# Attention scores and exponents as float32r limbs in 32-row tiles, with three exponent banks and one accumulator

## The chip, the cores and the metric

One core of one Trainium2 chip. The time is device microseconds of one launch; the figure of a kernel is the median of its runs. The kernel before took 2334.4 us (three runs, 2331.25 to 2337.49).

## What is computed

Four sequences of 1024 tokens with 128 features, all float32, go through four layers, each with a layer norm before it and a residual sum after it: attention a, a mixture of experts, attention b, and the same experts again.

```python
# attention a: 16 heads of 8
Q, K, V = (content @ W).reshape(b, n, 16, 8)          # for Wq, Wk, Wv
alpha = softmax(einsum('bqhd,bkhd->bhqk', Q, K) / sqrt(8))
alpha = where(causal, alpha, 0)                       # masked after the softmax
Y = einsum('bhqk,bkhd->bqhd', alpha, V)
# attention b: q and k turned by rotary tables, softmax over all keys, no mask,
# then an output projection with a bias
# experts: 8 routed SwiGLU experts, the best 2 per token by softmax + bias, and a shared one
```

In attention a the denominator of the softmax runs over all keys, also the masked ones.

## The kernel before, in words

`build` runs the stages one after another, each in a block of its own: `setup`, `project` and `attend` for a, `route` and `experts`, `project` and `attend` for b, `project_out`, `route` and `experts`. Engines are held together by semaphores alone.

**Groups.** A sequence's 16 heads are four groups (`g`) of four heads (`hh`); with four sequences a layer has 16 groups (`n`). `project` makes q and k in 8 chunks of 512 tokens, splits each into three bfloat16 parts (ScalarE copies, L464 and L468; VectorE's subtraction, L445; POOL's, L413), and SP stores the parts and v in DRAM (`store`, L366 to L378). `load_group` (L269) brings a group back: the parts of q and k stacked so that one matmul over 96 rows gives the sum of all products of parts. The 32 scores of group 0 are already made at the end of `project` (L503 to L509, and L448).

**Maxima.** `score` (L298): for a head and a tile of 128 queries two matmuls of 512 keys each into one of the two slots of `ps_two`, which VectorE reduces to the negated maximum over 1024 keys (`take_max`, L308). The 32 columns of maxima of a group are transposed (`turn_max`, L808), copied (L747), split into three bfloat16 parts by POOL (`split_max`, L658) and put by DMA as rows 96 to 98 beside q (L641); the matching rows of k hold ones. That way the second matmul (`exponents`, L863), keys on the output's partitions and 512 queries on its columns, gives score minus maximum.

**Exponentials and weighting.** ScalarE exponentiates each 128x512 result (L731) from two banks of `ps_one` into one of four buffers of `probs`. `weigh` (L841) multiplies v (8 columns, and a ninth of ones for the denominator) with it in float32, the four heads in the four 32-column strips of the array, 256 queries at a time, summed over all 8 key tiles in the two banks of `ps_sum`. In layer a the part below the diagonal needs the ones column alone (`w01`), POOL multiplies the diagonal tile with the causal mask (L687), and pairs of probability tiles are added by POOL (L677), so that one matmul does for both where only the denominator is wanted. ScalarE copies the sums (L718), TensorE transposes them (L815), VectorE divides (L753, L755) and adds or stores (L763, L765).

**Order.** TensorE's order is written out by hand in `body` (L849): per step one exponent matmul, then what stands in `uses` for the step (a unit of scores for a later group, 40 steps ahead; the sums; the maxima), the second exponent matmul, and a quarter of `weigh` of the key tile before. A group has 32 steps (`STEPS`). VectorE follows the same list. An exponent matmul waits for the exponential two before it (L862), a score for the reduction two before it (L803). SP loads the group three ahead once the group before has been weighed (L648, L649). The groups of one sequence are written out; over the sequences runs a loop (`over_groups`, L626), as over the chunks (`over_chunks`).

## Time and profile before

| | |
|---|---|
| median of three runs | 2334.4 us (2331.25 to 2337.49) |
| span of the profiled execution | 2335.9 us; no other time of this execution is given |
| instructions | 45054 |
| TensorE busy, matmuls | 2088.4 us, 89% |
| TensorE weight loads, beside them | 905.2 us, 39% |
| VectorE busy | 1747.2 us, 75% |
| ScalarE busy | 1402.6 us, 60% |
| POOL busy | 557.9 us, 24% |
| DMA | 69.96 MB, mean 30 GB/s |

How to read it: busy shares are means over stages with different limits. Matmuls are pipelined and their ends are modelled, so the distance between two starts tells more than a duration. L12 is line 12 of the kernel; PEld is TensorE's weight load, SPq the issue of a DMA by SP. In a line of the timeline, "x4" is a run of four instructions, the first number the start and the second the time that the run took.

### The profile page before, as it was taken

The page shows a single profiled execution, that of the slowest core. Times are in us where ns is not written, and L with a number is a line of the kernel's source. Part 1 is how long each engine was busy: PE and PEld are TensorE (multiplying, and loading weights), DVE is VectorE, ACT ScalarE, POOL GpSimd, SP SyncE. Part 2 cuts the span into 40 slices and gives each one's busy share as a digit, 9 for nine tenths or more (in the row PEclk, how much of TensorE's full clock was granted, in tenths as well). Part 3 has the DMA queues.
Part 4 walks back from the last instruction along what each step waited for, and adds up shares of the span by engine and source line. Part 5 has one row for each costly group of instructions (what it writes and reads, how often), then busy time and mean ns, then how long its engine had stood idle before and what let it go on. Part 6 is the DMA issues. An engine that isn't in the chain of part 4 may idle for free. (4 is left out here: it accounts for less than half of the span.)

```text
span 2335.9 us, 45054 instructions
## 1 busy us (share of the span) xinstructions
PE 2088.4 (89%) x15817; PEld 905.2 (39%) x16064; DVE 1747.2 (75%) x2442; ACT 1402.6 (60%) x2380; POOL 557.9 (24%) x579
## 2 busy tenths in 40 slices
PE   2689999999899999689975999999999999995999
PEld 1223333333333332478840223223222232225888
DVE  7687777778777873478887888878777888807777
ACT  1247776777677778422231677767777777782222
POOL 5234444454444455300052200000000000003000
PEclk9679999999999999689985899999999999996999
DMA  3510000100000000000024001100000010000000
GB/s 90 169 49 24 25 24 28 36 33 24 25 24 25 24 2 2 1 25 0 1 72 134 30 24 35 35 26 24 24 25 25 28 37 8 2 2 0 10 14 14
DMA packets 78586, 69.96 MB, mean 30 GB/s; under 512 B 40240, under 2 KB 73648, under 8 KB 73648
## 3 DMA queue, kind: packets, MB, share of 16 engines
q1 hardware_dynamic: 78384, 67.20, 8.9%
q8 instruction: 135, 2.21, 0.4%
q14 instruction: 67, 0.55, 0.1%
HBM read 47.52 MB, written 18.87 MB: 28 GB/s over the span
## 5 line engine op out<-in xcount | busy, mean ns | idle before, releaser
L308 DVE TENSOR_REDUCE b_negmax<-ps_two 128x1 f32<-128x1024 f32 x512 | 624.8, 1224 | 155.0 <-PE ps_two L300 154.8
L308 DVE TENSOR_REDUCE a_negmax<-ps_two 128x1 f32<-128x1024 f32 x512 | 617.3, 1222 | 154.8 <-PE ps_two L300 153.3
L731 ACT ACTIVATE at_probs<-ps_one 128x512 f32<-128x512 f32 x992 | 580.4, 597 | 243.3 <-PE ps_one L863 159.5
L300 PE MATMUL ps_two<-kx,qx 96*128 96x512 bf16 x2048 | 651.7, 402 | 79.6 <-DVE ap_rest L445 18.5
L731 ACT ACTIVATE bt_probs<-ps_one 128x512 f32<-128x512 f32 x992 | 588.4, 597 | 190.2 <-PE ps_one L863 156.9
L863 PE MATMUL ps_one<-qx,kx 128*128 128x512 bf16 x1746 | 670.9, 388 | 15.6 <-issue 8.1
L863 PEld LDWEIGHTS ps_one<-qx,kx 128*128 128x128 bf16 x1984 | 189.0, 96 | 539.5 <-issue 281.2
L841 PE MATMUL ps_sum<-bt_probs,vg 128*9 128x256 f32 x4096 | 322.3, 387 | 7.7 <-ACT bt_probs L731 0.6
L300 PEld LDWEIGHTS ps_two<-kx,qx 96*128 96x128 bf16 x2048 | 196.2, 100 | 236.8 <-DVE b_negmax L308 47.3
L687 POOL TENSOR_TENSOR at_pdiag<-at_probs,causal 128x512 f32<-128x512 f32 x128 | 162.5, 1269 | 359.6 <-ACT at_probs L731 359.6
L1172 ACT ACTIVATE xn<-ps_two 128x512 f32<-128x512 f32 x144 | 86.0, 597 | 234.8 <-PE ps_two L1141 234.8
L677 POOL TENSOR_TENSOR at_probs<-at_probs 128x512 f32<-128x512 f32 (+1 forms) x192 | 207.9, 1087 | 28.4 <-ACT at_probs L731 28.2
L663 POOL CAST bt_mparts<-bt_turned_max 32x128 bf16<-32x128 f32 x16 | 4.5, 279 | 762.0 <-DVE bt_turned_max L747 762.0
L1149 PEld LDWEIGHTS ps_one<-w,xt 128*128 128x128 f32 x1152 | 151.2, 192 | 13.4 <-DVE xt L1217 1.4
L1149 PE MATMUL ps_one<-w,xt 128*128 128x128 f32 x1152 | 152.4, 276 | 1.0 <-DVE xt L1217 1.0
L841 PEld LDWEIGHTS ps_sum<-bt_probs,vg 128*9 128x9 f32 x4096 | 69.7, 100 | 214.0 <-issue 207.6
L1217 DVE TENSOR_TENSOR xt<-xn,ps_two 128x512 f32<-128x512 f32 x144 | 98.8, 686 | 68.6 <-ACT xn L1172 66.7
L841 PE MATMUL ps_sum<-at_probs,vg 128*9 128x256 f32 (+1 forms) x2048 | 147.3, 360 | 1.2 <-ACT at_probs L731 0.6
L841 PE MATMUL ps_sum<-at_probs,w 128*9 128x256 f32 (+1 forms) x1920 | 135.3, 354 | 7.3 <-ACT at_probs L731 0.6
L262 PE MATMUL ps_one<-ident,xn 128*128 128x128 f32 x128 | 30.4, 385 | 86.7 <-DVE xn L251 86.2
L251 DVE TENSOR_SCALAR xn<-x,mean,rstd 128x128 f32<-128x128 f32 (+1 forms) x128 | 81.5, 809 | 8.6 <-PEq L1108 2.1
L1199 DVE SCALAR_TENSOR_TENSOR be_acc<-ps_one,be_gate,be_acc 128x128 f32<-128x128 f32 x288 | 80.6, 342 | 0.2 <-PE ps_one L1149 0.2
(147 smaller groups left out, 1606.9 us busy)
## 6 DMA issues: line engine op xcount, KB each, us to landing
qx<-qk_parts SPq DMA_DIRECT2D x96, 192.0 KB
kx<-qk_parts SPq DMA_DIRECT2D x96, 192.0 KB
qk_parts<-ap_parts SPq DMA_DIRECT2D x24, 256.0 KB, 2.8
qk_parts<-bp_parts SPq DMA_DIRECT2D x24, 256.0 KB, 2.6
vg<-v_rows SPq DMA_DIRECT2D x32, 128.0 KB
x<-in_x SPq DMA_DIRECT2D x4, 512.0 KB, 6.1
v_rows<-ap_vbuf SPq DMA_DIRECT2D x8, 256.0 KB, 2.7
v_rows<-bp_vbuf SPq DMA_DIRECT2D x8, 256.0 KB, 2.6
```

Of the source, the lines that this page charges most:

```text
L251: dve.tensor_scalar(m.xn[:, low % 2, t * P:(t + 1) * P], m.x[:, tile_cols(tile)], m.mean[:, bass.ds(tile, 1)], m.rstd[:, bass.ds(tile, 1)] ...
L300: last = pe.matmul(m.ps_two[:, slot, half * CHUNK:(half + 1) * CHUNK], m.qx[0:MAXROW, g, hh, i * P:(i + 1) * P], m.kx[0:MAXROW, g, hh, hal ...
L308: dve.tensor_reduce(sc.negmax[:, parity, hh * NT + i:hh * NT + i + 1], m.ps_two[:, slot, :], AX.X, ALU.max, negate=True).then_inc(sc.read, 1)
L677: pool.tensor_tensor(both, both, probs[:, jj % 4 - 1, hh, 0:shared(jj)], ALU.add).then_inc(paired, 1)
L687: pool.tensor_tensor(pdiag[:, jj % 2, :, :], probs[:, jj % 4, :, j * P:(j + 1) * P], m.causal[:, :].unsqueeze(1).to_broadcast([P, GH, P]), ...
L731: act.activation(probs[:, jj % 4, hh, half * CHUNK:(half + 1) * CHUNK], exponent_bank(n_left, hh, half), ACT.Exp, scale=SCALE).then_inc(ex ...
L841: last = pe.matmul(m.ps_sum[32 * hh:32 * hh + rows, half, q0 - half * CHUNK:q1 - half * CHUNK], w, src, start=clears and k == 0, stop=jj = ...
L863: pe.matmul(exponent_bank(n_left, hh, half), m.kx[:, g, hh, order[jj] * P:(order[jj] + 1) * P], m.qx[:, g, hh, half * CHUNK:(half + 1) * C ...
L1149: last = pe.matmul(m.ps_one[:, k % 2, t * D:(t + 1) * D], hid[:, k % 2, t * P:(t + 1) * P], m.w2[:, e, :], start=True, stop=True, skip_gro ...
L1172: act.activation(silu[:, k % 2, :], m.ps_two[:, k % 2, 0:CHUNK], ACT.Silu).then_inc(s_done, 1)
L1199: dve.scalar_tensor_tensor(part, m.ps_one[:, k % 2, t * D:(t + 1) * D], gate[:, h, t, e:e + 1], part, ALU.mult, ALU.add).then_inc(acc_done, 1)
L1217: dve.tensor_tensor(hid[:, k % 2, :], silu[:, k % 2, :], m.ps_two[:, k % 2, CHUNK:2 * CHUNK], ALU.mult).then_inc(a_done, 1)
```

## The change

q and k are kept as two float32r limbs (high, and the rest) in place of three bfloat16 parts. A head's operand is 24 rows: high x high, high x low, low x high, eight rows each. The four heads of a group lie in the four 32-row strips of `qx` and `kx`; the maxima follow as two rows (limbs) in each strip, beside ones in `kx`. Score and exponent matmuls are of 24 and 26 rows, in the strip of their head. The order is by steps again, but a step is: first score matmul, exponent matmul, second score matmul, exponent matmul; the heads are ordered so that neighbours are of different strips, and a score unit is one head by 1024 keys. The exponents go by blocks of one key tile and 512 queries for four heads, through three banks (both of `ps_one` and the second of `ps_sum`); `weigh` comes once in two steps with 512 columns, and one bank accumulates, which ScalarE copies twice per group. The scores run 44 steps ahead; the first 44 units come at the start of `attend`, after the loads of group 0, which are issued there. POOL's paired additions are gone. v goes into `vg` straight from ScalarE (four copies per chunk) and no longer over DRAM. The stored rows are 48 DMAs of 256 KB per layer. A group is loaded by eight DMAs (four heads, q and k), its maxima by eight. The loops over chunks and groups are written out in full, and the waits with a counter beside them (`hold`) are plain waits in `attend`. The diff, cut to its core:

```diff
-PARTS = 3
-PR = 32
-MAXROW = PARTS * PR
+PRODUCTS = 3
+ROWS = PRODUCTS * HD
+MAXROW = ROWS
+TILE_ROWS = 32
+LIMBS = 2
+SLOTS = 4
...
-    m.qx = sb("qx", [P, NG, GH, S], BF16)
-    m.kx = sb("kx", [P, NG, GH, S], BF16)
-    m.vg = sb("vg", [P, NG, NT, VW])
+    m.qx = sb("qx", [P, SLOTS, S], F32R)
+    m.kx = sb("kx", [P, SLOTS, S], F32R)
+    m.vg = sb("vg", [P, TILES, HEADS, HD + 1])
...
-            pool.memset(m.kx[:, :, :, :].bitcast(F32), 0.0).then_inc(cleared, 1)
...
+            pool.memset(m.kx[:, :, :].bitcast(F32), 1.0)
...
-def score(pe, m, sc, g, hh, i, slot):
-    for half in range(2):
-        last = pe.matmul(m.ps_two[:, slot, half * CHUNK:(half + 1) * CHUNK],
-                         m.qx[0:MAXROW, g, hh, i * P:(i + 1) * P],
-                         m.kx[0:MAXROW, g, hh, half * CHUNK:(half + 1) * CHUNK], start=True, stop=True)
-    last.then_inc(sc.filled, 1)
...
+            for chunk in range(CHUNKS):
+                b, h = divmod(chunk, HALVES)
+                slot = chunk % SLOTS
+                for limb, limb_done in ((0, high), (1, low_done)):
+                    sp.wait_ge(limb_done, chunk + 1)
+                    for c, order in enumerate(((0, 0, 1), (0, 1, 0))):
+                        for row in range(PRODUCTS):
+                            if order[row] == limb:
+                                sp.dma_start(m.qk_rows[b, c, row, :, h * CHUNK:(h + 1) * CHUNK].bitcast(F32),
+                                             limbs[:, slot, limb, c * CHUNK:(c + 1) * CHUNK].bitcast(F32)
+                                             ).then_inc(stored[slot], DMA)
+            for slot in range(SLOTS):
+                sp.wait_ge(stored[slot], DMA * 2 * PRODUCTS * (CHUNKS // SLOTS))
             if later:
...
+                    dve.tensor_tensor(limbs[:, t % SLOTS, 1, :], source(t % 2), limbs[:, t % SLOTS, 0, :].bitcast(F32),
+                                      ALU.subtract).then_inc(low_done, 1)
...
+                    for n in range(NG):
+                        last = act.activation(m.vg[:, chunk * CT:(chunk + 1) * CT, n * GH:(n + 1) * GH, 0:HD],
+                                              m.ps_sum[:, h, :].rearrange("p (t n d h) -> p t n h d", t=CT, n=NG, h=GH
+                                                                          )[:, :, n, :, :], ACT.Copy)
+                    last.then_inc(v_copied, 1)
...
+UNITS = NT * HALVES * 2
+EXPS = HALVES * NT * GH
+BLOCKS = HALVES * NT
+GROUPS = B * NG
+LEAD = 12
+SUMS_AT = 6
+PROB_SLOTS = 4
+E_BANKS = 3
+def tile_head_of(unit):
+    return unit // GH, (0, 2, 1, 3)[unit % GH]
+def ring_uses():
+    uses = {}
+    total = GROUPS * UNITS
+    for unit in range(total):
+        uses.setdefault(max(unit - UNITS - LEAD, -1), []).append(("scores", unit))
+        if unit % UNITS == 1 and unit >= UNITS:
+            uses[max(unit - UNITS - LEAD, -1)].append(("maxima", unit // UNITS - 1))
+    uses.setdefault(total - UNITS - LEAD + 1, []).append(("maxima", GROUPS - 1))
+    for n in range(GROUPS - 1):
+        uses.setdefault((n + 1) * UNITS + SUMS_AT, []).append(("sums", n))
+    uses.setdefault(GROUPS * UNITS, []).append(("sums", GROUPS - 1))
+    count = 0
+    out = {}
+    for step in sorted(uses):
+        out[step] = []
+        for kind, which in uses[step]:
+            out[step].append((kind, which, count))
+            count += 1
+    return out
...
+        e_banks = (m.ps_one[:, 0, :], m.ps_one[:, 1, :], m.ps_sum[:, 1, :])
+        acc = m.ps_sum[:, 0, :]
...
+        def pieces_of(j, half):
+            lo, hi, edge = half * CHUNK, (half + 1) * CHUNK, (j + 1) * P
+            if not masked_after or edge <= lo:
                 return [("all", lo, hi)]
+            if edge > hi:
+                return [("ones", lo, hi)]
+            return [("ones", lo, edge)] + ([("all", edge, hi)] if edge < hi else []) + [("diagonal", j * P, edge)]
...
+            def load_group(n):
+                b, g = divmod(n, NG)
+                if n >= SLOTS:
+                    sp.wait_ge(e_filled, EXPS * (n - SLOTS + 1))
+                for c, dst in enumerate((m.qx, m.kx)):
+                    for h in range(GH):
+                        sp.dma_start(dst[TILE_ROWS * h:TILE_ROWS * h + ROWS, n % SLOTS, :].bitcast(F32),
+                                     m.qk_rows[b, c, :, g * GR + h:(g + 1) * GR:GH, :].bitcast(F32)
+                                     ).then_inc(group_loaded[n % SLOTS], DMA)
+            def load_maxima(n):
+                for limb in range(LIMBS):
+                    sp.wait_ge(split, LIMBS * n + limb + 1)
+                    for h in range(GH):
+                        row = TILE_ROWS * h + MAXROW + limb
+                        sp.dma_start(m.qx[row:row + 1, n % SLOTS, :].bitcast(F32).rearrange("p (t q) -> p t q", q=P),
+                                     mlimbs[h * NT:(h + 1) * NT, limb, :].bitcast(F32)).then_inc(max_loaded, DMA)
+            for n in range(3):
+                load_group(n)
+            load_maxima(0)
+            for n in range(GROUPS):
+                if n + 3 < GROUPS:
+                    load_group(n + 3)
+                if n + 1 < GROUPS:
+                    load_maxima(n + 1)
...
+            for blk in range(GROUPS * BLOCKS):
+                if blk >= PROB_SLOTS:
+                    act.wait_ge(pv_done, blk - PROB_SLOTS + 1)
+                for k, h in enumerate((2, 3, 0, 1)):
+                    count = blk * GH + k
+                    act.wait_ge(e_filled, count + 1)
+                    act.activation(probs[:, blk % PROB_SLOTS, h, :], e_banks[count % E_BANKS], ACT.Exp, scale=SCALE
+                                   ).then_inc(exp_done, 1)
+                    if k == 1 and blk >= NT + 1 and (blk - 1) % NT == 0:
+                        copy_sums(*divmod((blk - 1) // NT - 1, HALVES))
+            copy_sums(GROUPS - 1, HALVES - 1)
...
-                def exponents(jj, hh, half):
-                    u = (n * STEPS + jj * GH + hh) * 2 + half
-                    if spare(n_left, hh) and jj == 0 and hh == 1:
-                        pe.wait_ge(two_read, uses_before(n, n_left, first))
-                    elif n_left == 1 and (jj or hh):
-                        pe.wait_ge(exp_done, u - 3)
-                    elif not (first and jj == 0 and hh == 0):
-                        pe.wait_ge(exp_done, u - 1)
-                    pe.matmul(exponent_bank(n_left, hh, half), m.kx[:, g, hh, order[jj] * P:(order[jj] + 1) * P],
-                              m.qx[:, g, hh, half * CHUNK:(half + 1) * CHUNK], start=True, stop=True
-                              ).then_inc(t_filled, 1)
...
+            def score(unit, half, slot, count):
+                n, u = divmod(unit, UNITS)
+                i, h = tile_head_of(u)
+                if half == 0:
+                    if u == 0:
+                        pe.wait_ge(group_loaded[n % SLOTS], DMA * LOADS * (n // SLOTS + 1))
+                    if count >= 2:
+                        pe.wait_ge(taken, count - 1)
+                rows = slice(TILE_ROWS * h, TILE_ROWS * h + ROWS)
+                done = pe.matmul(m.ps_two[:, slot, half * CHUNK:(half + 1) * CHUNK],
+                                 m.qx[rows, n % SLOTS, i * P:(i + 1) * P],
+                                 m.kx[rows, n % SLOTS, half * CHUNK:(half + 1) * CHUNK], start=True, stop=True)
+                if half:
+                    done.then_inc(filled, 1)
...
+            def exponents(blk, k):
+                n, half, j = blk // BLOCKS, blk % BLOCKS // NT, blk % NT
+                h, count = (2, 3, 0, 1)[k], blk * GH + k
+                rows = slice(TILE_ROWS * h, TILE_ROWS * h + MAXROW + LIMBS)
+                if count >= E_BANKS:
+                    pe.wait_ge(exp_done, count - E_BANKS + 1)
+                pe.matmul(e_banks[count % E_BANKS], m.kx[rows, n % SLOTS, j * P:(j + 1) * P],
+                          m.qx[rows, n % SLOTS, half * CHUNK:(half + 1) * CHUNK], start=True, stop=True
+                          ).then_inc(e_filled, 1)
...
+            def weigh(blk):
+                n, half, j = blk // BLOCKS, blk % BLOCKS // NT, blk % NT
+                b, g = divmod(n, NG)
+                pe.wait_ge(exp_done, GH * (blk + 1))
+                if j == 0 and blk:
+                    pe.wait_ge(acc_copied, blk // NT)
+                pieces = pieces_of(j, half)
                 for k, (kind, q0, q1) in enumerate(pieces):
                     if kind == "diagonal":
+                        pe.wait_ge(masked, diagonals(blk) + 1)
+                    width = HD if kind == "diagonal" else HD + 1
+                    for h in range(GH):
+                        w = m.w01[:, :] if kind == "ones" else m.vg[:, b * NT + j, g * GH + h, 0:width]
+                        src = (pdiag[:, diagonals(blk) % 2, h, :] if kind == "diagonal" else
+                               probs[:, blk % PROB_SLOTS, h, q0 - half * CHUNK:q1 - half * CHUNK])
+                        last = pe.matmul(acc[32 * h:32 * h + width, q0 - half * CHUNK:q1 - half * CHUNK], w, src,
+                                         start=j == 0 and k == 0, stop=j == NT - 1 and k == len(pieces) - 1,
+                                         skip_group_check=True)
+                last.then_inc(pv_done, 1)
...
+            ring(-1, 1)
+            for step in range(GROUPS * UNITS):
+                blk, part = divmod(step, 2)
+                ring(step, 0)
+                if step % UNITS == 0:
+                    pe.wait_ge(max_loaded, DMA * LIMBS * GH * (step // UNITS + 1))
+                exponents(blk, part * 2)
+                ring(step, 1)
+                exponents(blk, part * 2 + 1)
+                if part and blk:
+                    weigh(blk - 1)
+            weigh(GROUPS * BLOCKS - 1)
+            ring(GROUPS * UNITS, 1)
```

## Rows read from the trace of the kernel before

**Rows 1.** The page's parts 1 and 2: busy time and share; granted clock in 40 slices.

```profile
PE 2088.4 (89%) x15817; PEld 905.2 (39%) x16064; DVE 1747.2 (75%) x2442; ACT 1402.6 (60%) x2380; POOL 557.9 (24%) x579
...
PEclk9679999999999999689985899999999999996999
```

**Rows 2.** Windows: stretch, length, busy us of each engine, granted clock, DMA share, GB/s.

```profile
91.50:130.00 38.50, 32.90 (x64) 4.35 (x64) 37.41 (x32) 1.54 (x2) 4.00 (x2) 0.50 0.41 135
141.00:872.00 731.00, 690.78 (x6207) 239.44 (x6324) 577.48 (x562) 544.73 (x936) 350.49 (x351) 0.99 0.08 25
...
1297.00:2046.00 749.00, 723.89 (x5643) 221.97 (x5751) 590.87 (x528) 570.60 (x969) 19.50 (x56) 0.99 0.07 24
2048.00:2098.00 50.00, 45.98 (x431) 12.86 (x437) 2.28 (x7) 43.82 (x83) 1.39 (x4) 1.00 0.01 1
```

**Rows 3.** Waits from 1400 to 1900 us: total us, times, longest.

```profile
DVE b_negmax L308 <- PE ps_two L300: 106.3, 302, 4.6
ACT bt_probs L731 <- PE ps_one L863: 104.6, 321, 4.2
```

**Rows 4.** Timeline of VectorE at the end of projection a.

```profile
90.17 1.22 DVE L445 TENSOR_TENSOR ap_rest<-ps_two,ap_parts 128x1024 f32<-128x1024 f32 x1 [16.64 <-ACT ap_parts L464]
```

**Rows 5.** Timeline of one step in attention b.

```profile
1320.33 0.39 PE L863 MATMUL ps_one<-qx,kx 128*128 128x512 bf16 x1
...
1320.76 1.25 ACT L731 ACTIVATE bt_probs<-ps_one 128x512 f32<-128x512 f32 x2 [0.28 <-PE ps_one L863]
...
1320.99 0.38 PE L863 MATMUL ps_one<-qx,kx 128*128 128x512 bf16 x1
...
1321.30 0.63 PE L841 MATMUL ps_sum<-bt_probs,vg 128*9 128x256 f32 x8
...
1321.87 0.39 PE L863 MATMUL ps_one<-qx,kx 128*128 128x512 bf16 x1
```

**Rows 6.** Timeline of VectorE: starts and ends of both attentions, finishes of two groups.

```profile
92.59 37.66 DVE L308 TENSOR_REDUCE a_negmax<-ps_two 128x1 f32<-128x1024 f32 x32 [1.20 <-PE ps_two L300]
...
954.80 0.42 DVE L763 TENSOR_TENSOR x<-x,at_heads 128x256 f32<-128x256 f32 x1
...
1247.17 37.65 DVE L308 TENSOR_REDUCE b_negmax<-ps_two 128x1 f32<-128x1024 f32 x32
...
1972.73 0.35 DVE L753 RECIPROCAL bt_recip<-ps_two 128x32 f32<-128x32 f32 x1
...
2023.07 0.34 DVE L753 RECIPROCAL bt_recip<-ps_two 128x32 f32<-128x32 f32 x1
...
2097.86 0.29 DVE L765 COPY attn<-bt_heads 128x256 f32<-128x256 f32 x1
```

**Rows 7.** Exponentials in a row (timeline, last group); POOL's diagonal product (the page's part 5).

```profile
2078.83 1.09 ACT L731 ACTIVATE bt_probs<-ps_two 128x512 f32<-128x512 f32 x2
```

```profile
L687 POOL TENSOR_TENSOR at_pdiag<-at_probs,causal 128x512 f32<-128x512 f32 x128 | 162.5, 1269 | 359.6 <-ACT at_probs L731 359.6
```

**Rows 8.** Timeline of TensorE: transposes of the sums; float32r matmuls in the experts.

```profile
875.18 0.86 PEld L815 LDWEIGHTS ps_two<-ident,at_sums 128*128 128x128 f32 x8 [0.79 <-issue]
...
1005.48 0.47 PE L1141 MATMUL ps_two<-a_x_hi,a_w_hi 128*128 x1
...
1005.80 0.40 PE L1141 MATMUL ps_two<-a_x_lo,a_w_hi 128*128 x1
...
1006.03 0.40 PE L1141 MATMUL ps_two<-a_x_hi,a_w_lo 128*128 x1
```

**Rows 9.** Timeline of TensorE: score matmuls with nothing beside them.

```profile
93.87 2.17 PE L300 MATMUL ps_two<-kx,qx 96*128 96x512 bf16 x4 [0.47 <-DVE a_negmax L308]
```

**Rows 10.** Projections: VectorE's normalisations in a and b; a window with DMA full.

```profile
24.72 15.37 DVE L251 TENSOR_SCALAR xn<-x,mean,rstd 128x128 f32<-128x128 f32 x8 [2.01 <-PEq L187]
...
1203.48 4.96 DVE L251 TENSOR_SCALAR xn<-x,mean,rstd 128x128 f32<-128x128 f32 x4
```

```profile
65.00:70.00 5.00, 4.97 (x27) 3.23 (x25) 3.18 (x6) 4.09 (x6) 2.14 (x2) 1.00 1.03 329
```

521 lines of the change are left out of this document (132 added, 389 removed).

## The prediction

> **What bounds the kernel now.** I read the busy shares first, then windows by stage, then the waits. Over the span TensorE is busy 89%, VectorE 75% and ScalarE 60% [rows 1], which decides nothing, because stages with different limits are mixed. The windows set them apart [rows 2]: in the middle of attention b TensorE is busy 724 of 749 us, VectorE 591, ScalarE 571. The waits say the same [rows 3]: in 500 us VectorE waited 106 us for the score matmuls and ScalarE 105 us for the exponent matmuls. So in both attentions TensorE is the bound, and the reader should see that the other two are only 20% behind. The projections' ends are a different case: VectorE waits 17 us in a [rows 4], about as much in b, and then 32 score units run with nothing beside them.
>
> One step of attention b takes 1.54 us, from one exponent matmul (E) at 1320.33 to the one at 1321.87 [rows 5]. Between them start four 512-column matmuls, 0.22 us apart: E, two score matmuls, and E again at 1320.99 (3 x 0.22 later). The weighting matmuls (W: eight records, four heads side by side) start 0.31 us after that and hold the next back for 0.57. One W of 256 float32 columns is four passes, 1024 columns, 0.43 us at 2.4 GHz (the granted clock is full there, rows 2), so going into W and out of it costs 0.10 + 0.13 = 0.23 us. 4 x 0.22 + 0.43 + 0.23 = 1.54.
>
> From first reduction to last normalisation, attention a runs from 92.59 to 955.2 us, attention b from 1247.17 to 2098.2 [rows 6]: 863 + 851 = 1714 us. A whole group of b takes 50.3 us (reciprocals at 1972.73 and 2023.07).
>
> **The change, part by part.** *VectorE and ScalarE keep their work.* There are still 512 reductions of 1024 columns per layer, and 32 of them take 37.65 us when nothing holds them, 1.18 each [rows 6]. The finish of a group and the copy of its maxima hold VectorE for 1.6 us together (1972.73 to about 1974.1, and 0.3). A group's floor on VectorE is 32 x 1.18 + 1.6 = 39.3 us. Exponentials in a row take 0.545 us each (two in 1.09, rows 7), so ScalarE's floor is 64 x 0.545 + 2 x 0.545 = 36.0. The change touches neither floor.
>
> *TensorE.* Per block of two steps there are the same eight 512-column matmuls, now float32r, and one W of 512 columns in place of two of 256. Float32r matmuls with weights of their own follow each other after 0.23 us in the experts [rows 8], so the type costs 0.01 each against bf16. W is 0.85 + 0.23 per block against 2 x 0.66: half as many switches, 0.23 us less per block.
>
> *Do a score matmul and the exponent matmul behind it run side by side?* They lie in different 32-row strips of the array now. The trace has no row strips. The two ends are: in series, 0.23 us each; or wholly side by side, as the four column strips of W are (eight records, of 512 passed columns each, in 0.43 us; in series 1.7, rows 5). I take side by side: the nearest row is another division of the same array, and that overlaps fully.
> The Trainium skill (TensorE: Matmul & The Clock Gate, Part 3: Packing small matmuls) gives 3.07 times for four row tiles of 512 columns, not 4; no row here shows it. An estimate by that page puts a pair at 0.30 us, and the result near 2215.
>
> *Then the block hangs on a chain, not on TensorE's load.* There are three exponent banks for four E, so the fourth E waits for the first one's exponential. From E to the start of its exponential is 0.43 us (1320.33 to 1320.76, rows 5). A first float32r matmul after other work is followed after 0.32 us instead of 0.23 [rows 8], so I add 0.07: 0.50. The exponential 0.60, its signal 0.06 (a reduction from 92.59 to 93.81 releases a matmul at 93.87) [rows 6, 9], the fourth E 0.23, switch 0.10, W 0.85, switch 0.13: 2.47, with issue 2.5 us per block. TensorE's own queue is 4 pairs x 0.23 + 1.08 = 2.0, VectorE's 2.36, ScalarE's 2.18: all fit in.
>
> *Per group.* 16 x 2.5 = 40.0. One accumulator bank in place of two: twice a group W waits for its copy, behind which the queue stands, 0.75 each. The eight transposes of the sums, 0.86 [rows 8] and a switch: 1.1. The transpose of the maxima stands ahead of the next exponent matmul and waits for the reduction before: 1.1. That is 43.7 for b. In a, eight of sixteen blocks have 128 columns more for the diagonal, 0.21 each: 45.4. POOL's paired additions are gone with the waits on them, and the columns they saved are multiplied again, 9216 per head and group instead of 7936; both counts follow from the code and are inside these numbers. The diagonal product takes POOL 1.27 us [rows 7], beside W's first pieces of 0.85 and the exponent before; without that cover it would cost 0.4 per diagonal, 50 us in a.
>
> *Per layer.* 44 score units ahead of the first step at 1.18: 52. Then 468 steps, 14.6 groups: 639 (a: 664). Then 44 steps without scores, 22 blocks of 2.5, with copies and the end: 60 (a: 63). b 751, a 779, together 1530 against 1714: -184.
>
> *Projections.* SP issues 48 stores of 256 KB per layer, 12.6 MB, where it had 32, 8.4 MB; ScalarE waits for one of four buffers. DMA moved 329 GB/s when full [rows 10], so the stores take 38 us: hidden under eight chunks of 7 us in b, not in a. Removed in a are POOL's memset, under which eight of VectorE's instructions took 15.37 us [rows 10], and four memsets of qx; in both layers POOL's subtraction of the third part. In b a chunk takes 8.3 us, 4.96 of them in four normalisations beside POOL [rows 10]; without the second POOL operation I take 7.2. Gone too is the early load of group 0: now the stores land, the block ends, eight loads are issued and land, 8 us (an estimate) after the projection. The shorter work gives 15 to 20 in a and 9 in b; the late load and the fuller queue take back 8 to 15 each. I take -10 for both, between -30 and +40. Within the attentions SP's loads wait for a group that ended before and have 40 us of cover; the eight rows of maxima are issued 11 steps, 14 us, ahead. If that failed, TensorE would wait some 3 us per group. Writing the loops out I cost at nothing: issuing is not what any engine waits for in rows 3.
>
> **Sum.** 2335.9 - 184 - 10 = 2142 for the profiled execution, whose span is 1.5 above the median of 2334.4: I give 2141. Without the added 0.07 and with waits on banks hidden, a group is 41.5 and the time 2085. With one us per group more it is 2170.
>
> **Rivals.** *In series.* If row strips do not overlap, a block is 8 x 0.23 + 1.08 = 2.92 us, a group about 50 (a: 51.7) against 50.3 now; 842 + 870 = 1712 for the layers. The time is 2300 to 2350, 2328 in the middle. For it: no row shows row strips. Against it: the column strips.
> *DMA.* The projections become bound by their stores and the loads come late: 30 to 60 on the forecast, about 2190, still faster.
> *The clock, the other side.* With scores alone TensorE stays at half clock for 38 us (0.50, rows 2), although two matmuls of 512 columns at 1.2 GHz fill 0.85 of each 1.18 us, 73%. In the last group it stays at full clock with 0.85 of 1.09 us filled, 78%. After the change it is filled 0.92 + 0.85 of 2.5 us, 71%, much of it from strips of 24 rows. Should the clock stay at 1.2 GHz in the attentions, W is 1.7 us, a pair 0.46, a group 66 to 69, and the time about 2885; a quarter of the attention at half clock (190 of 743 us) eats the gain. Against it: at half clock the queue would be full, and a full queue was followed by full clock from 141 us on [rows 2].
> By the skill's page (Part 1: The HAM clock gate) the clock falls after an idle window; by that rule there is none here and the clock stays. The trace agrees for the last group.
> *It does not do what it says*: float32r in 24 rows at the rate of float32 would give some 2.9 ms; rows 8 speak against it.
>
> **Numbers.** Side by side, with the DMA case and partial overlap inside: 0.72, 2080 to 2240. In series 0.16, a third each below, within and above 0.3%. Clock or slow strips 0.12. 0.3% is 7 us, about what a measurement of this kernel can tell from no change. The range reaches into the series case, 2075 to 2345, and leaves out 0.12 above and 0.04 below. Faster 0.78, same 0.05, slower 0.17.
>
> **What would show it.** Right: score and exponent matmuls starting less than 0.05 us apart; VectorE busy near 90% in mid-attention and TensorE waiting for the other two; 43.7 us from one reciprocal to the next in b; scores in a beginning within 10 us of 91.5. Wrong: matmuls 0.23 apart throughout and groups of 50 us; a granted clock under 0.9 in the attentions; TensorE idle for over 20 us at a projection's end.

## Result, and the profile after

The changed kernel takes 2846.27 us (median of four runs, 2794.65 to 2880.27) against 2334.45 before: slower, ratio 1.2053, 95% interval 1.1968 to 1.2137. The interval rests on the two shorter runs; the four differ together with the clock, the longer the lower: 2794.65 us at a mean granted clock of 0.652, 2832.54 at 0.638, 2860.0 at 0.628, 2880.27 at 0.620. The profile shows the third of them.

The page's parts 1 and 2, to be held against [rows 1]:

```profile
span 2857.9 us, 33611 instructions
PE 2605.4 (91%) x12864; PEld 1127.3 (39%) x12864; DVE 1679.1 (59%) x2438; ACT 1261.3 (44%) x2412; POOL 282.6 (10%) x306
...
PEclk8585765656567656599955555555555555556699
```

VectorE, ScalarE and POOL all have less to do than before, and TensorE has 2953 matmuls fewer, but 517 us more busy time. The last line shows where to look: where the clock stood at 9 through both attentions, it now goes up and down between 5 and 8 in attention a (slices 2 to 16 of 71 us, counted from 0) and lies at 5 in b (slices 21 to 35). The experts between them (slices 17 to 19, 9) have their full clock.

Windows of the changed kernel in the columns of [rows 2]: mid-attention a, mid-attention b, two short stretches of a, the projection of a.

```profile
200.00:600.00 400.00, 385.90 (x2340) 144.95 (x2339) 244.53 (x243) 212.51 (x408) 69.83 (x66) 0.63 0.04 13
1600.00:2000.00 400.00, 391.59 (x1522) 123.53 (x1518) 223.71 (x206) 197.18 (x380) 4.43 (x12) 0.50 0.03 11
210.00:215.00 5.00, 5.00 (x33) 1.77 (x32) 4.41 (x5) 3.82 (x8) 0.00 (x0) 1.00 0.00 0
...
225.00:230.00 5.00, 5.00 (x23) 1.56 (x19) 2.51 (x3) 2.58 (x6) 0.00 (x0) 0.50 0.03 7
25.00:60.00 35.00, 25.77 (x120) 16.36 (x118) 14.84 (x28) 16.87 (x47) 0.00 (x0) 0.94 1.00 350
```

In b TensorE is filled for 392 of 400 us (98%), at 1.2 GHz. In a the clock alternates: 1.00 from 210 to 215 us, 0.50 from 225 to 230, with TensorE filled in both. Between the two lies the change from one group to the next, where W waits 0.57 us for the copy of the sums and the transpose of the maxima 1.07 us for a reduction. There TensorE is filled for 2.46 of 4 us, and the clock falls right after; the other falls looked at in a, up to 1000 us, lie at such changes of groups too. TensorE's W matmuls (L693) ahead of the change, and windows around it:

```profile
213.13 1.05 PE L693 MATMUL ps_sum<-at_probs,w 128*9 128x512 f32 x8
...
215.79 1.05 PE L693 MATMUL ps_sum<-at_probs,w 128*9 128x512 f32 x8
...
218.00:222.00 4.00, 2.46 (x17) 0.82 (x16) 3.06 (x4) 3.26 (x7) 0.00 (x0) 1.00 0.01 2
222.00:226.00 4.00, 3.89 (x17) 1.22 (x17) 1.61 (x4) 1.44 (x4) 0.74 (x2) 0.61 0.01 2
```

While the clock is full, a block of the changed kernel takes 2.66 us (213.13 to 215.79), against 2.5 in the forecast.

TensorE's timeline in attention b of the changed kernel, one block from one W (L693) to the next:

```profile
1699.49 1.90 PE L693 MATMUL ps_sum<-bt_probs,vg 128*9 128x512 f32 x8
1701.32 0.79 PE L650 MATMUL ps_two<-kx,qx 24*128 24x512 f32 x1
1701.32 0.79 PE L674 MATMUL ps_sum<-qx,kx 26*128 26x512 f32 x1
1701.33 0.79 PE L674 MATMUL ps_one<-qx,kx 26*128 26x512 f32 x1
1701.91 0.62 PE L650 MATMUL ps_two<-kx,qx 24*128 24x512 f32 x2
1702.34 0.62 PE L674 MATMUL ps_one<-qx,kx 26*128 26x512 f32 x1
1702.34 0.62 PE L650 MATMUL ps_two<-kx,qx 24*128 24x512 f32 x1
1702.86 0.79 PE L674 MATMUL ps_sum<-qx,kx 26*128 26x512 f32 x1
1703.59 1.90 PE L693 MATMUL ps_sum<-bt_probs,vg 128*9 128x512 f32 x8
```

A score matmul (L650) and an exponent matmul (L674) start in the same hundredth of a microsecond, so the row strips do run side by side. TensorE's steps take up to twice their time, though: W holds the next matmul back for 1.83 us (1699.49 to 1701.32) where the forecast had 0.98, a pair follows the pair before after 0.43 to 0.59, and the block takes 4.10 us instead of 2.5.

VectorE's first reductions and last finishes in the two attentions, answering to [rows 6] and, for the wait ahead of the first, to [rows 4]:

```profile
80.98 2.36 DVE L588 TENSOR_REDUCE at_negmax<-ps_two 128x1 f32<-128x1024 f32 x2 [28.14 <-PE ps_two L650]
...
1164.43 0.42 DVE L611 TENSOR_TENSOR x<-x,at_heads 128x256 f32<-128x256 f32 x1
...
1456.83 2.35 DVE L588 TENSOR_REDUCE bt_negmax<-ps_two 128x1 f32<-128x1024 f32 x2 [19.09 <-PE ps_two L650]
...
2622.24 0.29 DVE L613 COPY attn<-bt_heads 128x256 f32<-128x256 f32 x1
```

Taken to the end of each last instruction, these and [rows 6] split the profiled difference of 522.0 us (2857.9 - 2335.9). The projection of a ends 11.6 us earlier (80.98 against 92.59). Attention a takes 1083.9 instead of 862.6, +221.3. From a's end to b's first reduction it is 292.0 both times, 0.0. Attention b takes 1165.7 instead of 851.0, +314.7. The rest is 2.4 shorter. -11.6 + 221.3 + 0.0 + 314.7 - 2.4 = 522.0: all of the loss lies in the two attentions.

### The profile page after: what moved, and what is told of

The parts are those of the page before. It is cut to its first block and busy times, and to the rows that moved or that the text cites. A ratio compares the mean times of both kernels' runs of the same rounds, so it can differ in the third digit from the quotient of the medians.

```text
span 2857.9 us, 33611 instructions
## 1 busy us (share of the span) xinstructions
PE 2605.4 (91%) x12864; PEld 1127.3 (39%) x12864; DVE 1679.1 (59%) x2438; ACT 1261.3 (44%) x2412; POOL 282.6 (10%) x306
## 5 line engine op out<-in xcount | busy, mean ns | idle before, releaser
L650 PE MATMUL ps_two<-kx,qx 24*128 24x512 f32 x2048 | 850.4, 632 | 75.2 <-DMA kx<-qk_rows 54.9
L588 DVE TENSOR_REDUCE bt_negmax<-ps_two 128x1 f32<-128x1024 f32 x512 | 604.5, 1220 | 457.8 <-PE ps_two L650 457.8
L588 DVE TENSOR_REDUCE at_negmax<-ps_two 128x1 f32<-128x1024 f32 x512 | 604.3, 1220 | 380.8 <-PE ps_two L650 380.7
L674 PE MATMUL ps_one<-qx,kx 26*128 26x512 f32 x1366 | 727.0, 718 | 21.6 <-ACT at_probs L576 11.4
L650 PEld LDWEIGHTS ps_two<-kx,qx 24*128 24x128 f32 x2048 | 415.1, 294 | 761.3 <-DVE bt_negmax L588 382.4
L674 PE MATMUL ps_sum<-qx,kx 26*128 26x512 f32 x682 | 489.9, 718 | 12.1 <-ACT at_probs L576 6.8
L693 PE MATMUL ps_sum<-bt_probs,vg 128*9 128x512 f32 x2048 | 482.6, 1035 | 8.6 <-ACT bt_sums L568 8.6
L674 PEld LDWEIGHTS ps_one<-qx,kx 26*128 26x128 f32 x1366 | 279.6, 268 | 252.5 <-ACT bt_probs L576 105.9
L674 PEld LDWEIGHTS ps_sum<-qx,kx 26*128 26x128 f32 x682 | 182.7, 268 | 124.6 <-ACT bt_probs L576 53.1
L693 PE MATMUL ps_sum<-at_probs,w 128*9 128x512 f32 (+3 forms) x1536 | 223.1, 665 | 5.3 <-ACT at_sums L568 5.3
L693 PE MATMUL ps_sum<-at_probs,vg 128*9 128x512 f32 (+3 forms) x1280 | 206.3, 732 | 7.5 <-ACT at_sums L568 7.5
```

Source lines behind the costliest of these rows:

```text
L588: dve.tensor_reduce(negmax[:, n % 2, h * NT + i:h * NT + i + 1], m.ps_two[:, slot, :], AX.X, ALU.max, negate=True).then_inc(taken, 1)
L650: done = pe.matmul(m.ps_two[:, slot, half * CHUNK:(half + 1) * CHUNK], m.qx[rows, n % SLOTS, i * P:(i + 1) * P], m.kx[rows, n % SLOTS, hal ...
L674: pe.matmul(e_banks[count % E_BANKS], m.kx[rows, n % SLOTS, j * P:(j + 1) * P], m.qx[rows, n % SLOTS, half * CHUNK:(half + 1) * CHUNK], st ...
L693: last = pe.matmul(acc[32 * h:32 * h + width, q0 - half * CHUNK:q1 - half * CHUNK], w, src, start=j == 0 and k == 0, stop=j == NT - 1 and ...
```

## Experiments

Two theories stood first. **NARROW**: the clock falls because the 512-column matmuls now read 24 or 26 rows of the array; before they read 96 (scores) and 128 (exponents). **GAPS**: it falls because the new order (pairs, a chain over three banks) fills TensorE for less of the time. A filled share has to be read with care: at half clock TensorE's work takes twice as long, so the share rises once the clock is down. All kernels are compared with a run of the kernel before on the same chip, 2335.83 to 2336.94 us. Where nothing else is said, it is one run. The diffs are cut to their core.

**Few rows in the kernel before.** The order, type and count of the instructions stay; only fewer rows are read. Left out are the parts that hold the precision of q and k and the subtraction of the maxima.

```diff
+ROWS_USED = 24
...
-                         m.qx[0:MAXROW, g, hh, i * P:(i + 1) * P],
+                         m.qx[0:ROWS_USED, g, hh, i * P:(i + 1) * P],
...
-                    pe.matmul(exponent_bank(n_left, hh, half), m.kx[:, g, hh, order[jj] * P:(order[jj] + 1) * P],
+                    pe.matmul(exponent_bank(n_left, hh, half), m.kx[0:ROWS_USED, g, hh, order[jj] * P:(order[jj] + 1) * P],
```

> The kernel before with its order, waits and queues untouched; its score and exponent matmuls read 24 rows of the array (the high part of q by the three parts of k) in place of 96 and 128, so precision and the subtraction of the maxima are left out. Theory NARROW (the clock falls because the 512-column matmuls fill few rows of the array): the granted clock in both attentions falls from 0.99 to 0.5 to 0.65, a step of attention b goes from 1.53 us to about 2.8 (4 x 0.43 + 0.85 + 0.25), and the time from 2334 to over 3000 us. Theory GAPS (the clock falls because the changed order leaves TensorE with less of its time filled): order and filled time are those of before, so clock 0.99 and 2325 to 2345 us.

Measured: 3502.05 us. Windows of this kernel in mid-attention a and b:

```profile
300.00:1000.00 700.00, 696.22 (x3657) 178.72 (x3660) 335.99 (x328) 313.79 (x535) 200.91 (x201) 0.53 0.05 16
1900.00:2800.00 900.00, 897.26 (x3844) 188.03 (x3842) 395.56 (x353) 382.90 (x646) 13.92 (x40) 0.50 0.05 16
```

TensorE is filled over 99% of the time and has half its clock. Nothing of the change's order, types or banks is in this kernel. That is NARROW; GAPS, which had 2325 to 2345 us here, cannot give it.

**Few rows in the scores alone** (the first half of that diff; left out is the precision of the scores from which the maxima are taken):

> The kernel before with only the score matmuls on 24 rows (their precision is left out), the exponent matmuls on 128 as before. It asks whether the rows of some matmuls alone turn the clock. If the clock follows a mean of filled rows: half of the 512-column matmuls are narrow, the clock is between, and by the changed kernel's layers (0.63 in a, 0.50 in b) I expect 0.6 to 0.8 and 2600 to 3100 us; full clock and 2335 us if one wide kind is enough.

Measured: 3038.11 us, clock 0.74 from 250 to 900 us and 0.60 from 1700 to 2500. It lies between 2336.71 with all rows and 3502.05 with both kinds narrow: the exponent matmuls' 128 rows hold part of the clock. It is a matter of degree.

**All rows in the changed kernel.** Every score and exponent matmul reads 128 rows, so a result is the sum over four heads; the maxima are set to zero, and `qx` is cleared at the start.

```diff
-                rows = slice(TILE_ROWS * h, TILE_ROWS * h + ROWS)
+                rows = slice(0, P)
...
-                rows = slice(TILE_ROWS * h, TILE_ROWS * h + MAXROW + LIMBS)
+                rows = slice(0, P)
```

> The changed kernel with score and exponent matmuls over all 128 rows, so they can't run side by side; each result is then a sum over the four heads, and the maxima are zeroed. NARROW: the clock is back at 0.95 to 1.0 in both attentions, a group takes the 50 to 52 us of the series rival, the time is 2300 to 2370 us. GAPS: the same, since in series TensorE is filled (8 x 0.23 + 0.85 of 2.92 us). It tells the two apart only together with the kernel in one strip. If the clock stayed at 0.5, both would fall.

Measured: 2379.96 us, with the clock at 1.00 in mid-attention:

```profile
1400.00:2000.00 600.00, 582.95 (x3097) 299.38 (x3098) 454.24 (x421) 401.29 (x772) 8.13 (x24) 1.00 0.04 16
```

The time lies 10 us above the 2300 to 2370 expected.

**One strip for all heads.** Both slices begin at row 0 and have 24 and 26 rows, so nothing lies side by side and every head computes the first one's result.

> The changed kernel with all score and exponent matmuls in the first 32-row strip (24 and 26 rows): in series like the one with full rows, and as full in time, but narrow; all four heads then compute the first head's result. NARROW: clock about 0.5, a block of two steps 8 x 0.43 + 1.7 + 0.3 = 5.4 us, a group 88, the time about 3500 us (3300 to 3700). GAPS: clock 0.95 to 1.0 and 2300 to 2370 us, as with full rows.

Measured: 3625.81 us. Attention b:

```profile
2000.00:3000.00 1000.00, 1000.00 (x2907) 466.58 (x2899) 442.72 (x395) 426.32 (x722) 8.03 (x22) 0.50 0.03 9
```

TensorE has no gap at all in 1000 us, and half its clock. Between this kernel and the one with all rows, which has the same instructions and zeros for the maxima, lie 1246 us. The Trainium skill (TensorE: Matmul & The Clock Gate, Part 1: The HAM clock gate) has the clock set by how busy TensorE was; this trace, 100% filled at 0.50, agrees only if rows of the array are part of "busy".

**More narrow work.** The second score matmul of each unit is issued twice (the whole computation stays):

```diff
                 if half:
+                    done = pe.matmul(m.ps_two[:, slot, half * CHUNK:(half + 1) * CHUNK],
+                                     m.qx[rows, n % SLOTS, i * P:(i + 1) * P],
+                                     m.kx[rows, n % SLOTS, half * CHUNK:(half + 1) * CHUNK], start=True, stop=True)
```

> The changed kernel with every second score matmul issued twice into the same bank, same result: two more narrow matmuls per block, put where TensorE waits for the fourth exponent's bank, so that its waits in a block shrink. GAPS: the clock rises to 0.9 or more in the attentions and the time falls to 2150 to 2350 us. NARROW: the clock stays at 0.5 to 0.65 and the time is 2800 to 3150 us.

Measured: 2838.03 us, inside the changed kernel's own spread. In a the clock is 0.78 (200 to 1000 us), in b 0.50 (1600 to 2400). TensorE is filled for 96% and 97% of these stretches, as in the changed kernel (96% and 98%): at half clock its time was filled already. The run adds narrow matmuls and no filled share, so it says little against GAPS; in b the added matmuls don't bring the clock back, and whether they raised it in a, one run can't tell.

**Wider weights in W.** W's weights get 32 columns instead of 9, with the matmuls' rows and moving columns unchanged (the further columns are never read):

```diff
-                    width = HD if kind == "diagonal" else HD + 1
+                    width = HD if kind == "diagonal" else TILE_ROWS
```

> The changed kernel with the weighting matmuls' operand v (or ones) widened from 9 to 32 columns per head, the strip that it has anyway; the added results are not used and no matmul becomes longer. It asks whether columns of the array in use count beside rows. If they do: the clock in the attentions rises from 0.63 and 0.50 towards 1, and the time falls to 2150 to 2500 us. If only rows count: 2790 to 2880 us as before, clock 0.50 in b.

Measured: 2810.52 us, clock 0.70 in a and 0.50 in b. The time lies inside the changed kernel's spread: the columns that W uses are not what is missing.

**A wide filler.** One more matmul of 128 rows per block, written into the bank that the score matmul behind it overwrites:

```diff
+                if half and unit % 2 and count > UNITS:
+                    pe.matmul(m.ps_two[:, slot, half * CHUNK:(half + 1) * CHUNK],
+                              m.qx[:, n % SLOTS, i * P:(i + 1) * P],
+                              m.kx[:, n % SLOTS, half * CHUNK:(half + 1) * CHUNK], start=True, stop=True)
```

> The changed kernel with one more 512-column matmul over all 128 rows per block of two steps, into the score bank that is overwritten at once, where TensorE waits for a bank anyway. NARROW: rows in use rise by a wide matmul beside W; the clock is at 0.8 or more, a block is 2.5 to 3.0 us and the time 2200 to 2450 us. If one is too little, the clock stays at 0.5 in b and the time is 2850 to 3100. GAPS (already fallen for the narrow kernels in series) would see it as the doubled score, no change.

Measured: 2792.85 us, between the two outcomes expected, because a took one and b the other. Windows in a and b:

```profile
250.00:900.00 650.00, 625.71 (x5096) 262.70 (x5096) 501.23 (x510) 448.90 (x862) 151.23 (x144) 0.98 0.04 15
1600.00:2400.00 800.00, 800.00 (x2873) 247.78 (x2872) 413.59 (x369) 363.73 (x674) 8.04 (x22) 0.50 0.03 10
```

In a the extra work brings the clock back, 0.98 against 0.63, and a group takes 50.1 us instead of 64.1: more work, less time. In b TensorE is filled to the last and stays at 1.2 GHz, where the extra matmul only costs: 76.4 us per group instead of 68.5. One wide filler per block is enough in a and not in b.

**Two strips of 64 rows.** The changed kernel's data, read 64 rows at a time; a result is the sum over two heads, the maxima are zero, and `qx` is cleared at the start.

```diff
-                rows = slice(TILE_ROWS * h, TILE_ROWS * h + ROWS)
+                rows = slice(64 * (h // 2), 64 * (h // 2) + 64)
...
-                rows = slice(TILE_ROWS * h, TILE_ROWS * h + MAXROW + LIMBS)
+                rows = slice(64 * (h // 2), 64 * (h // 2) + 64)
```

> The changed kernel with two strips of 64 rows in place of four of 32: score and exponent matmuls of different strips can still run side by side, each result is a sum over two heads, the maxima are zeroed. NARROW: a pair then fills 128 rows instead of 50; the clock is 0.95 to 1.0, a block about 2.5 us, a group of b 43 to 46, and the time 2130 to 2230 us, what I had predicted for the change. If strips don't overlap at 64: 2380 us as with full rows. If the clock stays at 0.5: 2800 or more.

Measured: 2222.66 us, clock 1.00 in both attentions (200 to 700 and 1350 to 1850 us): under the kernel before.

**The same with the whole computation.** Each head gets a strip of 64 rows in one of two column ranges. Beyond its own 24 or 26 rows nothing is added: there q is zero, and from the strip's 33rd row on k is zero too. The two rows of maxima are cleared by transfers, four per group, before a slot's next scores. With two column ranges each there are three slots instead of four.

```diff
-SLOTS = 4
+SLOTS = 3
...
-    m.qx = sb("qx", [P, SLOTS, S], F32R)
-    m.kx = sb("kx", [P, SLOTS, S], F32R)
+    m.qx = sb("qx", [P, SLOTS, 2, S], F32R)
+    m.kx = sb("kx", [P, SLOTS, 2, S], F32R)
...
+                for h in range(GH):
+                    low = STRIP * (h // 2) + MAXROW
+                    sp.dma_start(m.qx[low:low + LIMBS, n % SLOTS, h % 2, :].bitcast(F32),
+                                 m.kx[TILE_ROWS:TILE_ROWS + LIMBS, n % SLOTS, 0, :].bitcast(F32)
+                                 ).then_inc(group_loaded[n % SLOTS], DMA)
...
-                rows = slice(TILE_ROWS * h, TILE_ROWS * h + ROWS)
+                rows = slice(STRIP * (h // 2), STRIP * (h // 2) + STRIP)
```

> The whole computation, with the strips of 64 rows made right: each head stands in the first 24 or 26 rows of a strip of 64 (heads 0 and 1 in the upper strip, 2 and 3 in the lower, the two of a strip in different columns), all other rows of the strip are zero in the weights, and every score and exponent matmul reads all 64 rows. Three groups' slots in place of four, and four short transfers of zeros more per group. The run with 64-row strips and data in all rows took 2222.66 us at a mean clock of 0.936. NARROW as rows read (what counts is how many rows a matmul spans, whatever stands in them): clock 1.00 in both attentions, blocks near 2.6 us, 2200 to 2270 us. NARROW as rows with data (what counts is how many rows do work on numbers that aren't zero): the clock stays near 0.50 to 0.75 in the attentions, as in the changed kernel, and the time is 2750 to 2900 us. If the transfers or the three slots hold it up, the clock is 1.00 and the waits on TensorE name the loads, 2270 to 2400 us.

Measured, five runs: 2238.79 us (2236.38 to 2241.14) against 2336.94; ratio 0.9577, 95% interval 0.9564 to 0.9591. It takes 4.2% less time than the kernel before, and does the whole computation. The clock is 1.00 in both attentions (200 to 700 and 1350 to 1850 us), so rows of zeros count for it. TensorE and ScalarE in attention b of this kernel, one block:

```profile
1601.32 1.04 PE L706 MATMUL ps_sum<-bt_probs,vg 128*9 128x512 f32 x8
...
1602.30 0.50 PE L663 MATMUL ps_two<-kx,qx 64*128 64x512 f32 x1
...
1602.30 0.49 PE L687 MATMUL ps_sum<-qx,kx 64*128 64x512 f32 x1
...
1602.63 0.39 PE L663 MATMUL ps_two<-kx,qx 64*128 64x512 f32 x1
1602.64 0.39 PE L687 MATMUL ps_one<-qx,kx 64*128 64x512 f32 x1
1602.90 0.60 ACT L589 ACTIVATE bt_probs<-ps_sum 128x512 f32<-128x512 f32 x1 [0.50 <-PE ps_sum L687]
...
1603.55 0.50 PE L687 MATMUL ps_sum<-qx,kx 64*128 64x512 f32 x1
...
1603.98 1.04 PE L706 MATMUL ps_sum<-bt_probs,vg 128*9 128x512 f32 x8
```

This is the chain of the forecast, link by link: exponent matmul at 1602.30, its exponential from 1602.90 to 1603.50, the fourth exponent matmul into the same bank at 1603.55, W at 1603.98. The block is 2.66 us (1601.32 to 1603.98), the same as the changed kernel's while its clock was full.

At a change of groups in a TensorE of this kernel waits as the changed one does, and is filled for 2.66 of 4 us, but the clock stays:

```profile
230.40:234.40 4.00, 2.66 (x16) 0.99 (x16) 3.06 (x4) 3.26 (x7) 0.00 (x0) 1.00 0.01 2
234.40:238.40 4.00, 3.85 (x26) 1.38 (x26) 2.88 (x5) 2.50 (x6) 0.73 (x2) 1.00 0.01 2
```

**How many rows read.** Two kernels change one number of the padded kernel, READ being 48 in one and 32 in the other; the rows left away held zeros.

```diff
-                rows = slice(STRIP * (h // 2), STRIP * (h // 2) + STRIP)
+                rows = slice(STRIP * (h // 2), STRIP * (h // 2) + READ)
```

> The padded kernel (2238.79 us), and only the number of rows that score and exponent matmuls read is changed, 64 to 48; the 16 rows left away held zeros. NARROW as a matter of degree (rows spanned): between full clock with 64 rows and half clock with 24 to 26. If 48 rows still suffice, 2235 to 2245 us at a mean clock of 0.93; if not, the clock alternates and the time is 2300 to 2800 us. If only the strip's size (64 rows of the array set aside) counts, whatever is read of it, 2239 us.

> The same with 32 rows read, still in strips that begin at rows 0 and 64. NARROW by rows read: close to the changed kernel, 2750 to 2900 us, clock 0.62 to 0.66. If only the division of the array counts (two places in place of four), 2239 us and clock 0.93. No rows with data are lost in either run, so a difference from 2239 us is due to rows of zeros that aren't read.

Measured: 2270.32 us with 48 rows and 2719.2 with 32; the first lies between the two outcomes expected, the second 31 us below its range. The 48-row kernel in mid-attention b and after VectorE's last reduction, which starts at 1943.7 us, where no score matmuls are left:

```profile
1450.00:1950.00 500.00, 476.41 (x2895) 169.34 (x2891) 421.34 (x391) 374.39 (x723) 8.12 (x22) 1.00 0.05 18
1945.00:1950.00 5.00, 4.19 (x29) 1.29 (x25) 0.28 (x1) 3.74 (x8) 0.73 (x2) 1.00 0.01 2
1950.00:1955.00 5.00, 3.97 (x26) 1.20 (x24) 0.00 (x0) 3.84 (x8) 0.00 (x0) 0.94 0.02 4
1955.00:1960.00 5.00, 4.68 (x20) 0.91 (x12) 0.00 (x0) 2.75 (x6) 0.00 (x0) 0.50 0.00 0
...
1985.00:1990.00 5.00, 3.97 (x28) 1.19 (x24) 0.00 (x0) 3.84 (x9) 0.00 (x0) 1.00 0.00 2
...
2000.00:2025.00 25.00, 22.80 (x73) 5.49 (x72) 0.00 (x0) 13.07 (x26) 0.00 (x0) 0.50 0.00 1
```

The 64-row kernel at the same place (last reduction at 1938.1), and the 32-row kernel in mid-attention b:

```profile
1945.00:1950.00 5.00, 3.97 (x24) 0.93 (x22) 0.00 (x0) 4.08 (x8) 0.00 (x0) 1.00 0.02 3
1950.00:1955.00 5.00, 3.98 (x28) 1.19 (x24) 0.00 (x0) 3.85 (x9) 0.00 (x0) 1.00 0.00 0
...
1968.00:2003.00 35.00, 27.10 (x157) 7.86 (x157) 0.69 (x2) 25.43 (x50) 0.00 (x0) 1.00 0.00 1
```

```profile
1450.00:1950.00 500.00, 492.89 (x1902) 192.07 (x1895) 279.20 (x258) 245.74 (x473) 5.14 (x14) 0.50 0.03 13
```

With 48 rows the full clock lasts while scores stand beside the exponents. Some 10 us after they run out it falls, comes back once (1985 to 1990) and falls again. With 64 rows it lasts to the end, although TensorE is filled no more than with 48 (3.97 and 3.98 of 5 us, against 4.19 and 3.97 with 48 ahead of the fall). With 32 rows it is gone throughout mid-attention b and is 0.85 in mid-attention a. Where the strip begins was the same in all three, so the division into two strips is not what counts. GAPS was wrong as the cause, since the same gaps leave the clock up when more rows are read. But gaps have a part where few rows are read: the falls with 48 rows, and those in attention a of the changed kernel, come where TensorE is filled less. At 48 rows the scores are gone there as well, and with them the second matmul beside each exponent matmul; no run keeps the two apart.

**The overlap.** The padded kernel with score and exponent matmuls put into the same strip:

```diff
-    return unit // GH, (0, 2, 1, 3)[unit % GH]
+    return unit // GH, (2, 0, 3, 1)[unit % GH]
```

> The padded kernel, all 64 rows read, with the heads' order of the score matmuls changed from 0, 2, 1, 3 to 2, 0, 3, 1, so that a score matmul and the exponent matmul beside it lie in the same strip of 64 rows. Nothing else changes. If the overlap of strips is what the chain forecast counted on, score and exponent matmuls now start 0.23 us apart, a block goes from about 2.65 to about 3.0 us, and the time is near the one with all 128 rows (2379.96): 2360 to 2410 us, clock 1.00 in the attentions. If the overlap is worth nothing: 2240 us.

Measured: 2360.77 us at full clock. TensorE's timeline in b:

```profile
1702.46 0.49 PE L663 MATMUL ps_two<-kx,qx 64*128 64x512 f32 x1
1702.80 0.39 PE L687 MATMUL ps_sum<-qx,kx 64*128 64x512 f32 x1
1702.99 0.49 PE L663 MATMUL ps_two<-kx,qx 64*128 64x512 f32 x2
1703.26 0.45 PE L687 MATMUL ps_one<-qx,kx 64*128 64x512 f32 x2
1703.55 0.39 PE L663 MATMUL ps_two<-kx,qx 64*128 64x512 f32 x1
```

The exponent matmul now starts 0.34 us after the score matmul, where the two started together. Taking these pairs apart costs 122 us (2360.77 - 2238.79), and the kernel is 1% slower than the one before even at full clock. The edit does not end all overlap: where one step's last exponent matmul meets the next step's first score matmul, the two are now of different strips. Seven matmuls start within 1.09 us (1702.46 to 1703.55), where the kernel with all rows, in which nothing can overlap, needs 1.50 (1602.20 to 1603.70 of its trace). So 122 us is the price of a part of the overlap.

In the table the filled share is TensorE's in mid-attention b. It is no higher in the kernels at full clock than in those at half clock; what sets these apart is the rows read.

| kernel | rows read (scores, exponents) | clock mid-a, mid-b | filled mid-b | us |
|---|---|---|---|---|
| before | 96, 128 | 0.99, 0.99 | 97% | 2334.4 |
| before, narrow scores | 24, 128 | 0.74, 0.60 | 96% | 3038.11 |
| before, both narrow | 24, 24 | 0.53, 0.50 | over 99% | 3502.05 |
| changed | 24, 26 | 0.63, 0.50 | 98% | 2846.27 |
| changed, one strip | 24, 26 | 0.50, 0.50 | 100% | 3625.81 |
| changed, strips of 64 | 64, 64 | 1.00, 1.00 | 95% | 2222.66 |
| padded, 32 read | 32, 32 | 0.85, 0.50 | 99% | 2719.2 |
| padded, 48 read | 48, 48 | 1.00, 1.00 | 95% | 2270.32 |
| padded, 64 read | 64, 64 | 1.00, 1.00 | 95% | 2238.79 |
| padded, same strip | 64, 64 | 1.00, 1.00 | 94% | 2360.77 |
| changed, all rows | 128, 128 | 1.00, 1.00 | 97% | 2379.96 |

## Why the prediction was wrong, point by point

**The step that failed is the clock.** The prediction held full clock in both attentions and set against the rival: "at half clock the queue would be full, and a full queue was followed by full clock from 141 us on". The queue did fill, 392 of 400 us in b, and the clock stayed at 0.50. A granted clock under 0.9 in the attentions was among the signs of being wrong. The full clock behind [rows 2] had come with matmuls of 96 and 128 rows; I read the share of filled time from the row and not how much of the array that time filled. The rival of the clock came near: it priced W at 1.7 us, a group at 66 to 69 and the whole at 2885. Measured: W 1.83 (with its switch); a group 68.5 in b, (2621.71 - 1594.2) / 15, and 64.1 in a, where the clock is 0.63; the time 2846. It had been given 0.12. Its main ground was the filled share of 71%, and "much of it from strips of 24 rows" stood beside it; the experiments bear out the second. That the time comes so near is in part luck, because the rival had half clock throughout, while a had full clock for part of the time. The comparison of filled shares misled as well. The last group at full clock with 78% filled has exponent matmuls of 128 rows. By the same count a block of b in the changed kernel is filled for 4 x 0.43 + 1.7 of its 4.10 us, 83%, and has half clock.

**Side by side**: right. Starts lie 0.00 to 0.01 us apart, in strips of 32 rows and of 64. The Trainium skill (TensorE: Matmul & The Clock Gate, Part 3: Packing small matmuls) has such tiles start together and gain less than their number. The padded kernel's trace agrees on the starts. For its two tiles it shows no loss of the gain: where nothing is waited for, a pair holds the next back for 0.24 us (1605.29 to 1605.53), about as long as a single matmul does. A pair behind W holds the next back for 0.33 us (1602.30 to 1602.63), as a first matmul did in [rows 8], not 0.23.

**The chain per block**: right in its links, 2.66 us against 2.5 at full clock, in the padded kernel and in the changed one while its clock was full. From matmul to exponential it is 0.60 instead of 0.50, and from the fourth exponent matmul to W 0.43 instead of 0.33. W with its switch is 0.98 (1601.32 to 1602.30), as forecast. A group of the padded kernel takes 45.1 in b and 47.0 in a, against 43.7 and 45.4. The attentions together take 1610.6 us there against the forecast 1530 and 1714 before, so even with the clock up the gain there is 103 us and not 184, and 2238.79 lies 98 above the forecast of 2141, at the edge of the 2080 to 2240 given for this case. The longer groups make up some 45 of the missing 81 us; the rest lies outside the fifteen full groups of each layer and was not taken apart.

**In series**: this rival was priced at 2328, with groups of 50 and 51.7. The changed kernel with all rows, in which nothing can overlap, has groups of 50.1 in b and 51.9 in a, the rival's own, and takes 2379.96 us. The padded kernel with its pairs apart has 48.7 and 50.7 and takes 2360.77. Its price of 2328 was still too low, and its own terms (1712 for the layers, -10 for the projections) add up to 2322.

**The projections**: -10 for the two together was forecast; measured are -11.6 for a and 0.0 for b. In a there is a gain, but DMA is full for 35 us (share 1.00, 350 GB/s) and VectorE then waits 28.1 us for the first scores, 19.1 in b. TensorE waits 28.8 us for the loads in a and 26.2 in b, where it had waited 15.7 before its first score matmul in b. In b its last projection matmuls end 8 us earlier, counted from the end of a, near the 9 forecast, and the longer wait took that back. The wait for the loads behind the stores was longer than the 8 us that I had given it. It was the sign of the DMA rival that I had named (TensorE idle over 20 us), but none of that rival's 30 to 60 us came, since the two stretches together came out as forecast.

**VectorE and ScalarE**: their floors hold. They are no bound in the changed kernel, busy 59% and 44% of the span; in the padded one VectorE is busy 82% (a) and 85% (b) of mid-attention, near the 90% I had named.

**What is left open.** How rows and filled time are weighed against each other was not measured, only these points. In a the falls come at changes of groups; why the clock rises again in a and not in b was not tried. a has more of W, which reads 128 rows, in its eight diagonal blocks, and the filler tipped a and not b, which fits but doesn't show it. All kernels but the changed, the padded and the one before ran once. Strips of 64 rows with other contents than one head and zeros, which would save the 16 KB of padding per partition, were not tried as a whole computation.

## What to carry to other kernels

Cutting a small contraction into narrow row strips saves TensorE's time only as long as the clock stays up: read the granted clock of the stretch together with the rows that its matmuls read, and don't take a filled queue as a promise of 2.4 GHz. Where a strip is narrow, read more rows of it, zeros if need be. At full clock matmuls of 48, 64 and 128 rows follow each other after the same 0.23 to 0.24 us, so the rows cost no time in a matmul; they cost room (16 KB per partition here) and the transfers that clear them. Here they turned a loss of 20.5% into a gain of 4.2%. Before a change to the shape of the hottest matmul, run the kernel before with that shape alone: the one edit that read 24 rows in it would have shown the loss.

## What the runs showed of the hardware that I had not expected

- The rows that the matmuls read move the clock, even with TensorE filled to 100%: 0.50 over 1000 us with 24 and 26 rows, 1.00 over 600 us with 128 in the same program but for zeros as maxima.
- Rows of zeros count for the clock: 2719.2 us with 32 read (0.50 in b), 2238.79 with 64 (1.00), the same data in both.
- More work can take less time: with a filler of 128 rows per block, a group of attention a takes 50.1 us instead of 64.1.
- Waits weigh more when few rows are read: at a change of groups, TensorE filled for 2.46 of 4 us, the clock falls with 24 and 26 rows; filled for 2.66 of 4 us it stays with 64.
- In the 48-row kernel the clock falls from 1.00 to 0.50 within some 10 us after attention b's last scores; in the 64-row kernel it stays at 1.00, with TensorE filled no more than there.
